# A fused two-layer transformer block: turning the row maxima earlier, turning the next input ahead of a product, one score bank ahead of the projections

## The reference, cut to what matters

```
x = x + linear_attention(layernorm(x))   # 16 heads of 8, q and k normalised
x = x + moe(layernorm(x))                # 8 experts, 2 taken, plus 2 shared
x = x + band_attention(layernorm(x))     # softmax(q k^T / sqrt(8)), 16 heads
x = x + expert_choice_ffn(layernorm(x))  # 16 experts, each takes 512 tokens
```

## Time and profile before

| | us |
|---|---|
| median of 3 runs | 1809.23 |
| the profiled execution | 1809.41 |
| its span, from the first to the last instruction | 1807.4 |
| PE busy | 1509.6 (84%) |
| DVE busy | 1187.1 (66%) |
| ACT busy | 859.7 (48%) |
| POOL busy | 546.6 (30%) |
| mean granted TensorE clock | 0.919 |

### The profile page before, as it was taken

How to read it: one execution, slowest core, us unless ns; L and a number is a source line. 1 busy time by engine, 2 the same in 40 slices (tenths; PEclk the granted TensorE clock), 3 DMA queues, 4 the chain that set the end, 5 groups by cost and what they waited for, 6 DMA issues and landing times.

```text
span 1807.4 us, 33637 instructions
## 1 busy us (share of the span) xinstructions
PE 1509.6 (84%) x10072; PEld 920.9 (51%) x10072; DVE 1187.1 (66%) x3463; ACT 859.7 (48%) x1787; POOL 546.6 (30%) x626
## 2 busy tenths in 40 slices
PE   2879999999999999999999999999988711447674
PEld 1445656565655556565656565655644311435563
DVE  5477778686878787777868687878756278801110
ACT  0426464646465555646464646555552522423331
POOL 1323222232313132323222231313130120058886
PEclk8879999999999999999999999999997855678888
DMA  2030221213030303031121303030302000044443
GB/s 73 1 82 25 65 55 42 63 32 86 9 88 7 87 16 85 27 68 51 44 57 38 83 13 88 7 87 16 79 26 65 17 2 1 7 93 81 98 84 60
DMA packets 83238, 90.70 MB, mean 50 GB/s; under 512 B 19520, under 2 KB 73024, under 8 KB 78528
## 3 DMA queue, kind: packets, MB, share of 16 engines
q1 hardware_dynamic: 71872, 80.76, 18.0%
q0 software_dynamic: 11264, 8.92, 3.6%
HBM read 58.95 MB, written 29.92 MB: 49 GB/s over the span
## 4 chain that ended last, share of the span: by engine, by line
PE 54%; DVE 17%; issue 12%; POOL 7%; DMA 3%; ACT 3%; SPq 1%; DVEq 1%; POOLq 0%; ACTq 0%
PE fa L702 7%; PE ba L608 6%; PE ba L603 6%; PE fa L694 6%; PE bo L861 6%; PE ba L614 5%; PE fa L712 4%; POOL out L573 3%; PE facc L712 2%; DVE passed L1496 2%; POOL got L543 2%; DVE nm L1286 2%; DMA QT<-nmT 2%; PE ba L981 1%; PE bo L770 1%
## 5 line engine op out<-in xcount | busy, mean ns | idle before, releaser
L1041 ACT ACTIVATE probs<-ba 128x512 f32<-128x512 f32 x640 | 349.6, 599 | 131.7 <-PE ba L614 129.5
L458 POOL TENSOR_TENSOR x<-x,gd 128x512 f32<-128x512 f32 x144 | 182.6, 1268 | 589.8 <-ACT gd L1019 573.3
L603 PE MATMUL ba<-QT,KT 75*128 75x512 bf16 (+3 forms) x1024 | 233.4, 306 | 26.1 <-ACT probs L1041 13.4
L608 PE MATMUL ba<-KT,QT 72*128 72x512 bf16 (+3 forms) x1024 | 230.4, 305 | 7.6 <-DVE nm L1289 3.2
L1286 DVE TENSOR_REDUCE nm<-ba 128x1 f32<-128x512 f32 x256 | 174.4, 681 | 34.2 <-PE ba L614 34.0
L861 PE MATMUL bo<-probs,vp 128*32 128x512 f32 (+3 forms) x2048 | 181.8, 444 | 2.0 <-ACT probs L1041 0.9
L603 PEld LDWEIGHTS ba<-QT,KT 75*128 75x128 bf16 x1024 | 87.5, 100 | 174.4 <-ACT probs L1041 103.4
L702 PE MATMUL fa<-f_nT,w 128*128 128x512 f32 x320 | 170.3, 614 | 3.4 <-DVE hh L1278 3.1
L694 PE MATMUL fa<-f_nT,w 128*128 128x512 f32 x320 | 169.6, 612 | 0.0
L614 PE MATMUL ba<-mask_q,identb 128*128 128x256 bf16 (+1 forms) x640 | 163.8, 256 | 0.0
L614 PE MATMUL ba<-mask_k,identb 128*128 128x256 bf16 (+1 forms) x640 | 163.5, 255 | 0.0
(11 more groups left out here) (279 smaller groups left out, 2668.1 us busy)
## 6 DMA issues: line engine op xcount, KB each, us to landing
QT<-qk_parts SPq DMA_DIRECT2D x96, 192.0 KB
KT<-qk_parts SPq DMA_DIRECT2D x96, 192.0 KB
qk_parts<-qkp SPq DMA_DIRECT2D x32, 384.0 KB, 2.6
fc<-in_L_ffn_fc_weight SPq DMA_DIRECT2D x32, 256.0 KB
xin<-in_L_attn_x SPq DMA_DIRECT2D x16, 256.0 KB, 7.4
qk_parts<-qkp SPq DMA_DIRECT2D x16, 256.0 KB, 2.7
out<-x SPq DMA_DIRECT2D x16, 256.0 KB, 2.3
xn_rows<-row SPq DMA_DIRECT2D x16, 256.0 KB, 7.2
```

Source lines behind the costliest of these rows:

```text
L458: pool.tensor_tensor(x1[:], x1[:], gd[:, e % 2], ALU.add).then_inc(S["s_x1g"], 1)
L603: pe.matmul(bank[:, col:col + w], lhsT=KT[0:K_ROWS, head, blk * P:(blk + 1) * P], rhs=QT[0:K_ROWS, head, blk * P:], start=first_, stop=False)
L608: pe.matmul(bank[:, col:col + w], lhsT=QT[0:QK_ROWS, head, blk * P:(blk + 1) * P], rhs=KT[0:QK_ROWS, head, 0:w], start=first_, stop=False)
L1041: act.activation(probs[:, pair % 3, f_], ba[n % 3][:], ACT.Exp, scale=SCALE).then_inc(S["s_exp"], 1)
```

## The change

Three edits, on PE and ACT alone. No instruction is added or taken away.

1. `turn_maxima(b, 0)` and ACT's copy of its result leave the end of the X phase. PE now turns behind the last fill of expert step e = 7, and ACT copies behind the scaling of step e = 8.
2. `f_turn_x(g)` stands ahead of `down(f, U0 - 1)`, which is down(9), and no longer behind it.
3. In the Y phase fill 0 stands ahead of the first call of `f_kvq`, and fills 1 and 2 behind it.

```
@@ PE, x_phase
                     if f is not None and e > 0:
                         down(f, e - 1)
                     next_fill()
-                if b is not None:
-                    turn_maxima(b, 0)
+                    if b is not None and e == 7:
+                        turn_maxima(b, 0)
+                if g is not None:
+                    f_turn_x(g)
                 if f is not None:
                     down(f, U0 - 1)
-                if g is not None:
-                    f_turn_x(g)
@@ PE, y_phase
+                fills(0)
                 if_f(f_kvq, 0)
-                fills(0, 1, 2)
+                fills(1, 2)
                 if_f(f_kvq, 1)
                 fills(3, 4)
@@ ACT, x_phase, inside the loop over e
-                if b is not None:
-                    copy(nmT[:, 0], bo[:].bitcast(BF16)[0:PARTS * HEADS // 2, 0:SEQ], "s_nmt", 2 * b + 1, "s_nmT")
+                    if b is not None and e == 8:
+                        copy(nmT[:, 0], bo[:].bitcast(BF16)[0:PARTS * HEADS // 2, 0:SEQ], "s_nmt", 2 * b + 1, "s_nmT")
```

## The result

The changed kernel took 1799.75 us (median of 5 runs, 1798.75 to 1801.12) against 1809.23 of the kernel before (here the median of 5 runs, 1808.16 to 1812.13, with the same median as the 3 runs given above): a ratio of 0.9944, 95% interval 0.9929 to 0.9958. That is 9.5 us less, where 13.9 were forecast; the time lies within 1788 to 1802, and 0.75 us above the forecast's own range of 1792 to 1799. The profiled execution's span fell from 1807.4 to 1797.8 us.

The account below looks back on a forecast made before the run. PE's products were taken to lead the chain, with the maxima's DMA in it. 14 boundaries at 0.75 us (10.5), batch 14's 0.1 and batch 15's 3.3 sum to 13.9 us off, forecasting 1795.3 us, range 1788 to 1802.

Parts of the forecast that it names:

- What bounds the kernel: Chain of PE products containing the maxima's DMA, 2% of the span; hiding that transfer shortens each X and Y boundary.
- What is late next: At loop boundaries, the fourth projection waits about 1.1 us for DVE's first bias addition, behind x3 and its statistics.
- The size at one boundary: Each of 14 loop boundaries gets 0.75 us shorter, following DVE's 0.74; bounds -0.33 and 1.42.
- x3 starts at 406.80: On DVE, x3 starts 0.16 us behind POOL's last addition, at 406.80 instead of 407.54, so 0.74 us earlier.
- the turn's price: The maxima's turn in its new place on PE delays what follows, including down(7) and POOL's addition of it, by 0.33 us.
- The idle takes up the turn: PE's 0.34 us of idle at the last two fills absorbs the turn's 0.33; down(8) keeps its start, down(7)'s addition does not.
- Batch 14: Boundary without a next input: fills start 3 us earlier but r_turn waits for normalised x3; gain 0.1 us, at most 3.0.
- Batch 15: Last batch, without an expert step: fill 0 starts earlier, gaining 3.3 us, between 3.0 and 3.6; below, 0.
- fill 0 can start when DVE's last maxima are done: In batch 15, fill 0 starts at 1395.7, plus up to 0.54 us if the turn at low clock delays the maxima.
- More: Rival: DVE's line is not the limit; 1.15 us a boundary, 19.5 us in all, 1790 us; chance 0.16.
- less: Rival: the Y phase gives part back as ACT's row keeps its place; 0.3 us a boundary, 1801.6 us; chance 0.12.
- The clock: Rival: PE's idle in one 1.1 us piece lowers the clock, up to 2.8 us a fall; slower, chance 0.05.

Follow-up runs that it names:

- Short last addition: On the changed kernel, POOL's last addition adds only 8 of 128 columns, leaving the rest of down(8) out of x3: 1783.98 us, ratio 0.9855.
- turn behind down(7): Against the kernel before: maxima turned behind down(7) in step 8, copied in step 9, input turned early, projections still ahead of fill 0: 1797.33 us, ratio 0.9931.
- turn twice: On the changed kernel, the turn of the first half's maxima is done twice over in step 7: 1802.54 us, ratio 0.9954 to the kernel before.
- turn alone: Against the kernel before, only the maxima's turn moves to step 7 and its copy to step 8: 1798.9 us, ratio 0.9936.
- edits 1 and 2: Against the kernel before, maxima and input are turned early, but fill 0 stays behind the projections: 1799.47 us, ratio 0.9936.
- input alone: Against the kernel before, only the input's turn moves ahead of down(9); the maxima are turned at the end as before: 1810.7 us, ratio 1.0004.

## Why the prediction was right in kind and high in size

- **What bounds the kernel, and that hiding the transfer shortens every step: right.** Fill 0's waits went, 15 of 16, and the step is shorter in every round of the loop.
- **What is late next: right, and this is what held the gain down.** The forecast had the fourth projection wait about 1.1 us for the bias; the row shows 1.11. That match is partly luck. PE is further ahead than forecast, since down(8) and down(9) take 403.27 - 402.38 = 0.89 and 404.60 - 403.71 = 0.89 us to their followers, where the forecast took 0.98 and 0.99; counted its way, with 0.67 us for the third projection, the wait is 408.80 - (406.83 + 0.67) = 1.30. The profile counts the idle from that projection's own end, 0.86 us behind its start. The forecast had x3 set by POOL's last addition, in a row with the one before it. Short last addition and turn behind down(7) show it by taking it away.
- **The size at one boundary, 0.75 forecast, 0.55 at x3 and 0.60 in the step (84.084 - 83.487 before rounding): too high.** The term that failed is "x3 starts at 406.80". Its first part is the turn's price, taken as 0.33 us from its start to its follower's. The turn also delays itself: from the mask ahead of it to its start it is 397.53 - 397.32 = 0.21 us, where a fill follows after 0.11. down(7)'s addition came 0.43 late (402.96 - 402.38 = 0.58 behind down(8)'s start, against 403.71 - 403.56 = 0.15), not 0.33. Its second part is the gap between two additions in a row on POOL, taken as 0.07; two of 1.27 and 1.26 us take 2.68, so it is 0.15. Together 0.18 of the 0.19 us.
- **The idle takes up the turn: right for down(8), and as foreseen not for down(7).** From down(7) to down(8) it is 402.38 - 400.57 = 1.81 us now and was 403.56 - 401.32 = 2.24, so the idle between them took up the turn's 0.43 whole. The forecast charged the rest to POOL, and turn twice shows the rate: nearly one for one.
- **Edits 2 and 3: the working followed them in full, but gave them no worth of their own, and they have none in the loop.** What I did not say is that they could be left out. PE's lead at the third projection, 1.8 us in the forecast, is (410.00 - 403.56) - (406.83 - 402.38) = 2.0 behind down(8); all of it beyond what x3's line gives is spent in front of the bias. (410.00 is the third projection's start before.)
- **Batch 14, 0.1: right.** x3 there comes no earlier, and its turn takes over the wait, 3.03 us:

```profile
1328.12 1.11 PE L636 MATMUL facc<-ident,b_n 128*128 128x128 f32 x4 [3.03 <-DVE b_n L1175]
```

- **Batch 15, 3.3: too high, 1.9 from the last x3 to the end.** Up to fill 0 the gain is (1399.27 - 1331.07) - (1389.15 - 1323.39) = 2.4 us. Fill 0 and the last maxima now (PE, then DVE):

```profile
1389.15 0.58 PE L603 MATMUL ba<-QT,KT 75*128 75x512 bf16 x1 [0.98 <-DMA QT<-nmT]
```

```profile
1388.32 0.68 DVE L1292 TENSOR_REDUCE nm<-ba 128x2 f32<-128x512 f32 x1
```

  The wait is put down to the DMA, which came last, but fill 0 also waits for all maxima, and these were done only at 1388.32 + 0.68 = 1389.00, 0.15 us before it. So the step "fill 0 can start when DVE's last maxima are done" held to 0.15. What failed is when they are done: 1389.00 - 1323.39 = 65.61 us behind the last x3, against 1395.67 - 1331.07 = 64.60 before. That is 1.0 later, where the forecast allowed 0.28. About 0.4 of it arises behind the turn, which delays the last five fills (DVE stood idle 0.24 us at 1385.75 for a fill). The other 0.6 was there before the turn: DVE stood idle 0.23 and 0.38 us for fills at 1368.71 and 1371.75, in a spell of low clock (0.66 in the mean from 1366 to 1369) that the trace before does not have at that place (1.00).
- **How firm the 1.9 is: not very.** Each figure is one trace. The kernels with the same order in batch 15 give, from the last x3 to the end, 474.4 us (the change), 476.1 (turn alone), 476.0 (edits 1 and 2) and 475.0 (turn twice), against 476.3 before and with input alone: a gain of 0.3 to 1.9 (2.4 with the short last addition). In the change, 0.64 us more was lost behind fill 0, where the low clock lasted longer; the same products took 0.87 us before and 0.85 with the turn alone, and 1.51 here:

```profile
1399.54 1.51 PE L861 MATMUL bo<-probs,vp 128*32 128x384 f32 x8
```

  Why the clock fell and rose at other moments from trace to trace is open.
- **The rest of the difference is the start**, -0.6 us up to the first x3, where only edit 2 applies. Over the kernels of this study the first x3 stood at 79.5 to 81.5 us, with edit 2 and without it.
- **The rivals.** "More" is refuted by the waits; "less" is nearer in time (1801.6) than the forecast (1795.3), but had the wrong mechanism, for ACT's row moved with DVE's: its squares start 414.27 - 407.54 = 6.73 us behind x3 before and 412.49 - 405.81 = 6.68 now. The clock did not fall in the loop: 1.11 us of idle in one piece left it at the high level, 1.00 from 404 to 412 us.

So in these two traces 14 boundaries gave 8.3 instead of 10.5, batch 15 gave 1.9 instead of 3.3, and the start took 0.6.

## What to carry to other kernels

When a wait is taken away at a place where several lines meet, find the line that is late next and price it instruction by instruction, with the gaps between dependent ones; what is gained is its slack and not the idle removed. A small step moved forward on a full engine delays all that follows there: look behind which of its products another engine's chain hangs, and put the step behind that one. Try each part of a change by itself: here one of three did the whole work, and the best place for it was one product later.

## What the runs showed of the hardware

- Two dependent additions in a row on POOL have 0.15 us between them, though one engine runs both (2.68 us for 1.27 + 1.26).
- Four small transposes on PE cost 0.43 us where they stand alone between other work, 0.10 of it ahead of them; a second pass of four right behind costs 0.23.
- After batch 14's boundary the clock fell whether PE's idle stood in front of fill 0 (2.99 us, before) or in front of x3's turn (3.03 us, after): there the matmuls of fills 5 to 7 take 0.63 us where the others take 0.38. Before the change fills 0 to 4 still ran at the high level behind the idle (0.39), and the maxima's turn at 1334.66 was the first at the low one (0.60 against 0.39). That is the rule of the Trainium skill (TensorE: Matmul & The Clock Gate, "Why this matters for your kernels") that idle between bursts brings the lower clock, and the trace agrees; in the loop 1.11 us did not.
- At the first boundary of all, where PE has less work, the low level followed shorter idles too: before the change 0.43, 0.69, 1.69 and 0.67 us between 78 and 86 us, and then x3's turn took 1.09 us where it takes 0.65 in the loop (PE):

```profile
85.93 1.09 PE L636 MATMUL facc<-ident,b_n 128*128 128x128 f32 x4 [0.67 <-DVE b_n L1174]
```
